# Keeping the slopes of the fourth sweep in SBUF: a chord step in a gated recurrence

## The reference, cut to what matters

```python
def _L0_cond2_ref(h_t, z, W, b, alpha):
    Wh, Wz = W[:, :D], W[:, D:]
    leak = 1.0 - alpha
    def step(h, z_t):
        gate = jax.nn.sigmoid(h @ Wh.T + z_t @ Wz.T + b)
        h_new = jnp.tanh(h * leak + gate * z_t)
        return (h_new, h_new)
    _, hs = jax.lax.scan(step, h_t, jnp.swapaxes(z, 0, 1))
    return jnp.swapaxes(hs, 0, 1)
```

## Time and profile before

| | us |
|---|---|
| median of 3 runs (1027.6 to 1031.14) | 1030.26 |
| the profiled execution, its time | 1030.18 |
| the profiled execution, span of the core | 1028.4 |
| busy: PE, DVE, ACT, POOL over the span | 732.3, 658.8, 511.9, 257.2 |
| the recurrence: first matmul of sweep 1 to the verdict | 616.8 to 773.4 |

### The profile page before, as it was taken

One profiled execution on the slowest core, in us unless ns is written; L12 is line 12 of the kernel. 1 busy time (PEld: TensorE's weight loads), 2 busy tenths in 40 slices (PEclk: granted clock), 3 DMA queues, 4 the chain that ended last, 5 costly groups with the idle time before them and its releaser, 6 DMA issues. The chain is left out here.

```text
span 1028.4 us, 15090 instructions
## 1 busy us (share of the span) xinstructions
PE 732.3 (71%) x5686; PEld 456.6 (44%) x5686; DVE 658.8 (64%) x950; ACT 511.9 (50%) x832; POOL 257.2 (25%) x231
## 2 busy tenths in 40 slices
PE   3830029786664478839758389999966689999995
PEld 1310015334554467735425144444425447766773
DVE  5999959778547883575696527999990422333331
ACT  6878646565224336555344248999970212232221
POOL 0000000001101000001403305999880033334331
PEclk9975559899898588988778699999985589999998
DMA  5620000005950000011000074000006611111100
GB/s 200 246 84 0 0 21 0 1 0 135 252 144 4 2 3 24 3 24 72 0 0 1 0 262 167 1 1 1 0 0 227 232 39 40 41 40 39 42 11 1
DMA packets 35882, 60.69 MB, mean 59 GB/s; under 512 B 8187, under 2 KB 22523, under 8 KB 35426
## 3 DMA queue, kind: packets, MB, share of 16 engines
q1 hardware_dynamic: 30194, 51.31, 15.6%
q0 software_dynamic: 3312, 6.31, 2.0%
q10 hardware_dynamic: 2304, 2.10, 0.6%
HBM read 55.23 MB, written 7.21 MB: 61 GB/s over the span
## 5 line engine op out<-in xcount | busy, mean ns | idle before, releaser
L1861 ACT ACTIVATE moe_ht<-x_tr,moe_b 128x128 f32<-128x128 f32 x184 | 50.3, 385 | 147.1 <-PE x_tr L1826 147.1
L1817 PE MATMUL x_y<-moe_w,moe_ht 128*128 x368 | 85.0, 385 | 2.1 <-ACT moe_ht L1861 2.1
L1808 PE MATMUL x_hid<-w,moe_xt 128*128 x184 | 85.6, 609 | 0.9 <-DVE moe_xt L1951 0.7
L1140 POOL TENSOR_TENSOR path<-path,mix_pr 128x1280 f32<-128x1280 f32 x16 | 38.3, 2422 | 152.2 <-DVE mix_pr L1302 152.2
L1817 PEld LDWEIGHTS x_y<-moe_w,moe_ht 128*128 128x128 f32 x368 | 69.4, 193 | 11.6 <-issue 2.8
L1958 DVE COPY moe_hid<-x_hid 128x512 f32<-128x512 f32 x46 | 31.9, 692 | 64.4 <-PE x_hid L1808 64.4
L216 PE MATMUL bad_sum<-spike_bad,ones 128*128 128x16 f32 x2 | 0.6, 384 | 85.1 <-ACT spike_outside L182 85.1
L1470 PE MATMUL r_bank<-recur_h_other,recur_wg 128*128 128x512 f32 x128 | 60.2, 592 | 0.0
L1466 PE MATMUL r_bank<-recur_zw,eye 128*128 128x512 f32 x112 | 57.2, 592 | 0.8 <-ACT recur_zw L1501 0.8
L212 PE MATMUL w_bank<-spike_wbuf,spike_pick 128*128 128x512 f32 x80 | 39.1, 645 | 22.4 <-DMA spike_wbuf<-in_gW 22.4
L474 DVE SCALAR_TENSOR_TENSOR proj_y<-proj_pre,mix_st,proj_y 128x1024 f32<-128x1024 f32 x36 | 46.2, 1284 | 11.0 <-ACT proj_y L437 9.8
(11 more groups left out here) (282 smaller groups left out, 1839.4 us busy)
## 6 DMA issues: line engine op xcount, KB each, us to landing
spike_wbuf<-in_gW SPq DMA_DIRECT2D x8, 1280.0 KB, 6.1
w<-in_w1T SPq DMA_DIRECT2D x8, 1024.0 KB, 12.6
moe_w<-in_w2T SPq DMA_DIRECT2D x8, 1024.0 KB, 10.7
fir_band<-in_band_l SPq DMA_DIRECT2D x11, 512.0 KB
fir_band<-in_band_m SPq DMA_DIRECT2D x11, 312.0 KB
mix_st<-in_band_l SPq DMA_DIRECT2D x5, 512.0 KB
xT<-in_xT SPq DMA_DIRECT2D x4, 512.0 KB, 6.3
xT<-in_xT SPq DMA_DIRECT2D x2, 1024.0 KB, 6.0
```

The costliest lines, as they stand in the source:

```text
L1140: nc.gpsimd.tensor_tensor(x, x, w, ALU.mult).then_inc(s.weighted, 1)
L1808: last = nc.tensor.matmul(hid_bank[n][:], xt[:, c, :], m.w1[:, bass.ds(e, 1), c, n * N:(n + 1) * N].rearrange("p o n -> p (o n)"), start=( ...
L1817: last = nc.tensor.matmul(y_bank[:], ht[:, k, :], w2[:, bass.ds(e, 1), k, :].rearrange("p o n -> p (o n)"), start=(k == 0), stop=(k == K2 ...
L1861: nc.scalar.activation(ht[:, k, :], tr_bank[k // (K2 // 2)][:, k % (K2 // 2) * P:(k % (K2 // 2) + 1) * P], ACT.Relu, bias=b1[:, bass.ds(e, ...
```

## The change

The first three sweeps (u = 0 to 23) stay as they are. In the fourth (u = 24 to 31) ScalarE writes the slope into a new SBUF buffer `kept` of 8 units instead of into PSUM. In sweeps 5 to 7 (u = 32 to 55) ScalarE issues neither the Square nor the Identity, and the scans read `kept` again. So 48 of ScalarE's instructions go, and 32 scans, those of u = 24 to 55, have the slope from SBUF. No semaphore's count is waited for that was not there before.

```diff
+    KEPT = 3
...
+    DRAWN = (KEPT + 1) * UNITS
...
         change = sb("change", [P, UNITS, N])
+        kept = sb("kept", [P, UNITS, N])
...
+        def slopes(u):
+
+            return j_bank[u % RING][:] if u < KEPT * UNITS else kept[:, u % UNITS, :]
...
                 nc.scalar.activation(out, step[:, u % UNITS, :], ACT.Square).then_inc(s.sq_ready, 1)
                 act.wait_ge(s.sq_ready, u + 1)
-                nc.scalar.activation(out, out, ACT.Identity, bias=leak[:, c:c + 1],
+                nc.scalar.activation(slopes(u), out, ACT.Identity, bias=leak[:, c:c + 1],
                                      scale=leak_neg[:, c:c + 1]).then_inc(s.j_ready, 1)
...
                     value(u - LAG_F)
-                    slope(u - LAG_F)
+                    if u - LAG_F < DRAWN:
+                        slope(u - LAG_F)
...
-                dve.wait_ge(s.j_ready, u + 1)
+                dve.wait_ge(s.j_ready, min(u + 1, DRAWN))
                 dve.wait_ge(s.res_ready, u + 1)
                 if t0:
                     dve.wait_ge(s.change_ready, u - C + 1)
-                nc.vector.tensor_tensor_scan(change[:, r, :], j_bank[u % RING][:], rest[:, r, :], first,
+                nc.vector.tensor_tensor_scan(change[:, r, :], slopes(u), rest[:, r, :], first,
                                              ALU.mult, ALU.add).then_inc(s.change_ready, 1)
```

## The result

The changed kernel is slower: 1050.25 us against 1028.93 in the median of four runs each, ratio 1.021 (95% interval 1.016 to 1.026). The forecast was 1054 us, range 1040 to 1066. The profiled execution took 1047.75 us with a span of 1046.0, 17.6 us over the span before. The change's own cost is larger than that: the stages ahead of the recurrence, which are the same in both, happened to be 3.45 us shorter in this execution (first sigmoid at 617.60, before at 621.05). I therefore compare one stretch in all kernels, from the first sigmoid of the sweeps to the start of the verdict's last instruction: 152.2 us before, 173.1 after, so 20.9 us. From there to the end it is 255.2 and 255.3 us. All of the loss is in the sweeps.

What follows compares the result with a forecast made beforehand. TensorE bounded the sweeps; turns between scan and GpSimd would take over. 103.5 + 0.3 - 2.2 - 77.3 = 24.3 us, less 0.1, on 1030.2 gave 1054 us, range 1040 to 1066.

Steps and rivals of the forecast that it cites:

- TensorE is the bound: In all seven sweeps TensorE sets the pace, 2.577 us a unit, so removing 32.4 us of ScalarE's work buys nothing.
- The 0.1 us at the end: At the last scan, no longer waiting for the Identity of u = 55 gains 0.1 us (0 to 0.3).
- The scan's own duration from SBUF: In the 32 scans, reading the slope from SBUF adds nothing by itself: 1.279 against 1.277 us with a start value.
- The scan takes turns with GpSimd: From u = 24, scans with two SBUF inputs alternate whole instructions with GpSimd's SBUF reads; 24.3 us slower, chance 0.78.
- Rival A: Scans take no turns with GpSimd; TensorE stays the bound, time 1030.1 us, not slower; chance 0.12.
- E: ScalarE's free time does speed the sweeps through some unseen wait, 1 to 3 us less, 1028; chance 0.02.
- B: Scan and GpSimd share SBUF partly, period about 2.9 us, some 11 us slower, 1041; chance 0.04.
- The period: From u = 24, one scan and two GpSimd instructions in turn, less 0.27 saved at the changes: 3.34 us a unit.
- The edges: First scan's wait adds some 0.3 us; fewer GpSimd instructions between the last scans save about 2.2.
- The clock: TensorE's gaps in the slowed sweeps leave it 77% busy at full clock, so nothing is counted.
- Rival C: TensorE's gaps cost it the clock in the sweeps, 1065 to 1085 us; chance 0.03.
- D: Last sweep's residual misses 1.6e-5 and engines walk 1024 steps one by one, at least 0.7 ms; chance 0.01.

Runs made afterwards that it cites:

- e2: Changed kernel with its scans reading the PSUM banks' last drawn slopes, Square and Identity still left out from the fifth sweep; stretch 152.2 us, ratio to before 0.9999.
- e7: On top of e3, ScalarE sums the last sweep's squared residuals for the verdict, replacing VectorE's 8 reductions; ratio to before 0.9951, stretch 148.2 us.
- e6: Changed kernel with GpSimd's residual and move from the fourth sweep on replaced by write-only fills of 1024 columns; ratio 0.998, stretch 151.9 us.
- e5: Changed kernel with GpSimd's residual and move cut to 256 of 512 columns from the fourth sweep on; ratio to before 1.001, stretch 153.0 us.
- e1: Changed kernel with slopes drawn anew into SBUF in every sweep, so ScalarE keeps all its work; ratio to before 1.020, stretch 173.1 us.
- e4: Changed kernel keeping the sixth sweep's slopes, so 16 scans read SBUF, not 32; ratio to before 1.008, stretch 163.2 us.
- e3: Changed kernel keeping squares in SBUF; Identity makes slopes into PSUM every sweep and scans read PSUM; ratio to before 1.000, stretch 152.2 us.

## Why the prediction was right

- **TensorE is the bound, ScalarE's 32.4 us buy nothing.** Shown: e2 takes them away alone and the stretch stays at 152.2. The 0.1 us at the end was not seen; the last scan waits for its residual instead, 0.21 us in e2 as in e7, as the text had it. One reading of the text is not quite so and changes nothing: ScalarE's sigmoids lie 2.98 to 2.42 us apart at the start of the first sweep too (622 to 633 us), not only at 670.
- **The scan's own duration from SBUF is the same.** Shown by e6, 1.218 against 1.217 us, and by e5's median.
- **The scan takes turns with GpSimd.** Shown: with GpSimd's work as it is, 1.9 us (changed kernel, e1, e4); with half of it, 1.22 (e5); with writes in place of reads, 1.22 (e6). Rival A falls with this, and E with e2. B, the partial sharing, falls with the two scans of 742.34 and 745.72, which end 1.08 us behind the residual however long they were beside it; its period was to be 2.9 us, and 3.20 is measured.
- **The period.** Predicted 3.34, measured 3.20. This term was mis-sized, by what the turns save. At the change to the scan the text took off 0.14, and measured is 0.14 or 0.20: the scans end 1.08 us behind GpSimd, alone they take 1.22, or 1.28 with a start value. At the change back it took off 0.13, and measured is 0.20: the move of 743.31 ended 0.89 behind the scan and that of 746.32 ended 1.06 behind, where moves take 1.09 or 1.27 alone. And GpSimd's residual is recorded from 0.04 before the move's end, which the text had not counted. In the mean 1.08 + 0.97 + 1.18 - 0.04 = 3.19. Over 31 periods the difference of 0.14 makes 4.3 us.
- **The edges.** Up to the start of the last scan their total was right: 31 periods of 3.20 are 99.3 us, and from the scan of u = 24 to that of u = 55 it took 97.3, which is 2.0 less where 1.9 was forecast. The two parts were not right, and that they cancel is luck. At the start the text added 0.3 us, and the first two distances took 5.98 us, 0.4 less than two of 3.20. At the end 1.6 us were saved and not 2.2, since the last scan waited 1.15 us for its residual. And that scan itself, for which the text counted nothing, took 2.21 us and not 1.28: GpSimd did two instructions and not one between the last two scans. So the loss is 97.3 - 77.3 = 20.0 us up to the last scan, against 24.3 forecast, and 0.9 behind it.
- **The clock.** No cost, as counted: 1.00 in windows with TensorE at 17.1 of 20 us (85%, where 77% was forecast), and the experts' stage took 255.3 us, before 255.2. Rival C fell, though its sign as the text words it, a clock under 0.9 between 690 and 790, did show: 0.78 in 760 to 780. The sweeps' last matmul ended at 769.1; up to 770 the clock is 1.00, and from 772 on it is 0.50 (1.2 GHz), with no matmul left to slow but the verdict's. Before, it ended at 761.3 and the clock is 0.50 from 766 on, and the verdict's matmul takes 0.59 us in both.
- **The verdict.** The bound was met; D did not happen, in the changed kernel nor in e3 or e7 with the same slopes.

The rule of the Trainium skill that the prediction set beside the trace (SBUF — State Buffer, Who interferes with whom) held in all its parts that the experiments tried. By its part on instructions that only write, e6 should have been free of the wait, and the trace agrees. That whole instructions wait, and not shares of them, agrees too, within the 0.2 us at each change. The same section makes an exception for VectorE's 2-port modes, which `tensor_scalar` can enter with one SBUF input; the prediction's wording leaves it out, and one row at the end of this text may fall under it.

## What to carry to other kernels

Before moving an operand, count the SBUF inputs of the VectorE instruction that reads it: for the scan here the second one cost nothing while GpSimd only wrote (1.218 us), and it cost a wait for a GpSimd instruction each time where GpSimd read SBUF nearly all the time (1.9 us). A longer duration in a row of busy time can be a wait; compare the same line's duration between operand forms before calling the engine slow. And when the relieved engine is not the bound, look for what its free time could take over elsewhere, as in e7, rather than for a gain where it was.

## What the runs showed of the hardware that was not expected

- The comparison in e7 (L1621, 8 columns, SBUF to SBUF) took 1.01 us from 762.53 to 763.54, where the same instruction took 0.17 with GpSimd idle (L1607 before). The second of GpSimd's three moves ended at about 763.55 (761.19 + 2 x 1.18). So an instruction with one SBUF input seems to take a turn too when it is a `tensor_scalar`; this rests on one instruction and was not isolated. VectorE's reductions before (L1604, one SBUF input too) were not held up: 0.66 to 0.68 us each, the first ones beside GpSimd's last moves and the later ones with GpSimd idle.
- ScalarE's Identity took 0.787 us from SBUF in e3 and e7's later sweeps against 0.750 from PSUM.
- GpSimd's residual at full width took 1.09 us for units with even u and 1.27 for odd ones (the two halves of the channels), in all kernels; no run here tells why.
